# The next group's q1 turn in an attention loop: from a group's third step into its first

## The reference

```python
qkv = jnp.einsum('bsd,df->bsf', x, Wqkv) + bqkv
q, k, v = ...                       # 32, 8 and 8 heads of 8
k = jnp.repeat(k, N_REP, axis=2)    # N_REP = 4
v = jnp.repeat(v, N_REP, axis=2)
scores = jnp.einsum('bqhd,bkhd->bhqk', q, k) / np.sqrt(HEAD_DIM)
attn = jax.nn.softmax(scores, axis=-1)
out = jnp.einsum('bhqk,bkhd->bqhd', attn, v).reshape(bsz, seqlen, D_MODEL)
return jnp.einsum('bsd,de->bse', out, Wo) + bo
```

## Time and profile before

| | |
|---|---|
| median of 3 runs | 671.64 us (670.51 to 672.01) |
| profiled execution | 669.68 us |
| its span | 667.8 us, mean granted TensorE clock 0.986 of 2.4 GHz |
| attention loop of layer 1 | about 362 to 563 us in the span |
| TensorE busy (matmul) | 617.4 us, 92% of the span |
| VectorE busy | 404.4 us, 61% |
| ScalarE busy | 325.1 us, 49% |
| 256 maxima (L1744) | 681 ns each |
| 256 exponentials (L1505) | 598 ns each |

### The profile page before, as it was taken

The page is one execution under the profiler, slowest core; times in us unless marked ns, Lnnn a source line. Parts: engine busy times, 40 slices in busy tenths (PEclk is TensorE's granted clock), DMA queues, the critical chain, the costliest instruction groups (busy, mean ns, idle before and its releaser), DMA issues.

```text
span 667.8 us, 11795 instructions
## 1 busy us (share of the span) xinstructions
PE 617.4 (92%) x4298; PEld 408.0 (61%) x4298; DVE 404.4 (61%) x929; ACT 325.1 (49%) x645; POOL 213.2 (32%) x312
## 2 busy tenths in 40 slices
PE   3999999999999988799978999999999999989990
PEld 2887887887888785366665544444444445546660
DVE  4526705632760587533366999989998954743336
ACT  4523423433332224133215589898988875523322
POOL 5870561282073154513333031201010100331331
PEclk9999999999999999899989999999999999999996
DMA  6000200300199992222379994000000000031213
GB/s 220 33 1 33 96 1 20 107 1 1 38 283 299 78 314 77 78 58 81 105 237 346 303 180 3 1 1 2 2 1 2 1 2 1 9 104 55 81 56 126
DMA packets 69000, 57.40 MB, mean 86 GB/s; under 512 B 21520, under 2 KB 64400, under 8 KB 68944
## 3 DMA queue, kind: packets, MB, share of 16 engines
q1 hardware_dynamic: 66736, 50.60, 31.2%
q0 software_dynamic: 2208, 6.05, 2.5%
HBM read 30.78 MB, written 25.85 MB: 85 GB/s over the span
## 4 chain that ended last, share of the span: by engine, by line
PE 73%; DVE 16%; DMA 3%; ACT 3%; issue 2%; POOL 1%; SPq 1%; ACTq 0%; POOLq 0%; DVEq 0%
PE psum L303 9%; PE psum L305 8%; PE psum L304 8%; PE psum L1289 8%; PE psum L1634 8%; DVE mx L1744 7%; PE psum L1606 5%; PE psum L1318 5%; PE psum L1594 5%; PE psum L1619 3%; PE psum L1213 2%; DVE stat L666 2%; PE psum L1564 2%; PE psum L1282 2%; PE psum L1199 1%
## 5 line engine op out<-in xcount | busy, mean ns | idle before, releaser
L1744 DVE TENSOR_REDUCE mx<-psum 128x1 f32<-128x512 f32 x256 | 157.6, 681 | 17.6 <-PE psum L1606 17.5
L1505 ACT ACTIVATE pr<-psum 128x512 f32<-128x512 f32 x256 | 138.0, 598 | 27.9 <-PE psum L1619 26.1
L1634 PE MATMUL psum<-pr,vals 128*32 128x256 f32 x1024 | 77.6, 389 | 0.0
L1619 PE MATMUL psum<-qT,kT 32*128 32x512 f32 x256 | 76.6, 494 | 0.7 <-ACT pr L1505 0.7
L1606 PE MATMUL psum<-kT,qT 32*128 32x512 f32 x256 | 67.7, 488 | 1.7 <-ACT qT L1472 0.7
L1289 PE MATMUL psum<-w_gu,xgT 128*128 x120 | 56.4, 592 | 0.0
L624 POOL DMA_INDIRECT routed_y<-yr,xg x30 | 28.7, 958 | 86.1 <-DVE yr L876 85.5
L1606 PEld LDWEIGHTS psum<-kT,qT 32*128 32x128 f32 x256 | 26.3, 181 | 43.9 <-issue 21.4
L1546 POOL CAST mp<-mx 128x16 bf16<-128x16 f32 x16 | 3.1, 196 | 150.5 <-DVE mx L1744 150.5
L867 DVE SCALAR_TENSOR_TENSOR h<-psum,xg,sg 128x256 f32<-128x256 f32 x30 | 14.5, 484 | 49.8 <-ACT sg L1046 49.8
L1046 ACT ACTIVATE sg<-psum,xg 128x256 f32<-128x256 f32 x30 | 14.2, 474 | 60.4 <-PE psum L1289 60.4
(11 more groups left out here) (214 smaller groups left out, 1406.6 us busy)
## 6 DMA issues: line engine op xcount, KB each, us to landing
sorted_x<-zeros SPq DMA_DIRECT2D x2, 9088.0 KB, 39.2
w_gu<-in_L_ffn_gate_w SPq DMA_DIRECT2D x16, 256.0 KB, 6.2
w_gu<-in_L_ffn_up_w SPq DMA_DIRECT2D x16, 256.0 KB, 6.3
w_d<-in_L_ffn_down_w SPq DMA_DIRECT2D x16, 256.0 KB, 6.6
xg<-sorted_x SPq DMA_DIRECT2D x30, 129.0 KB, 2.2
wk_f<-in_L_attn_Wk SPq DMA_DIRECT2D x4, 512.0 KB, 5.2
wq_f<-in_L_attn_Wq SPq DMA_DIRECT2D x4, 512.0 KB, 6.0
wv_f<-in_L_attn_Wv SPq DMA_DIRECT2D x4, 512.0 KB, 3.7
```

Of the source, the lines that this page charges most:

```text
L1505: nc.scalar.activation(pr[d % 3][:, j], s2_bank(d, j), ACT.Exp, scale=SCALE).then_inc(exp_ready, 1)
L1619: mm(s2_bank(d, j), kT[n // GH][rows, kc * P:(kc + 1) * P], qT2[n % 2][rows, :], start=True, stop=True).then_inc(s2_made, 1)
L1634: last = mm(ps[AV_BANK][j * VW:(j + 1) * VW, cols], vals[:, n // NKV * TB + kc, n % NKV // GH * GH + j, :], pr[d % 3][:, j, cols], start=( ...
L1744: v.tensor_reduce(mx[n % 2][:, t, j:j + 1], s1_bank(c, j), AX.X, ALU.max, negate=True).then_inc(max_read, 1)
```

## The change

`turns_at` gave `q1` of the next group in a step 2, by itself. It now gives it in a step 0, ahead of the `o` turn. `q2` (step 1), `k` (step 3) and `o` (step 0) stay. For the first groups this means that `q1` of group 1 goes from step 2 to step 0, that of group 2 from step 6 to step 4, and so on to group 15, from step 58 to step 56. TensorE's and ScalarE's order and the ring `FOR_ACT` follow; VectorE's, GpSimd's and SyncE's orders are the same. The number of instructions is the same.

```diff
@@ -1369,14 +1369,14 @@
         def turns_at(c):
 
             if c % TB == 0:
-                what = ("o", (c - 12) // TB)
+                what = [("q1", c // TB + 1), ("o", (c - 12) // TB)]
             elif c % TB == 1:
-                what = ("q2", (c - 5) // TB)
-            elif c % TB == 2:
-                what = ("q1", c // TB + 1)
+                what = [("q2", (c - 5) // TB)]
+            elif c % TB == 3:
+                what = [("k", (c + 5) // 16 if (c + 5) % 16 == 0 else NG)]
             else:
-                what = ("k", (c + 5) // 16 if (c + 5) % 16 == 0 else NG)
-            return [what] if 0 <= what[1] < (NKT if what[0] == "k" else NG) else []
+                what = []
+            return [x_ for x_ in what if 0 <= x_[1] < (NKT if x_[0] == "k" else NG)]
```

## The result

The changed kernel takes 667.52 us (median of 20 runs) against 672.15 for the kernel before in the same comparison: ratio 0.9927, 95% interval 0.9908 to 0.9947, so 3.6 to 6.2 us less. The forecast was 667.8 us, 3.8 less than the 671.64 that it started from. That 667.8 and 667.52 lie so close is in part luck: 671.64 was the median of 3 runs, and the median of 20 is 0.5 higher. The profiled execution took 665.95 us, with a span of 664.2 against 667.8.

A forecast was written before the change was run, and what follows sets the result against it. Bound by the order of waits among three nearly full engines, step 2 paced by TensorE, step 0 by VectorE. 10 x 0.40 + 2 x 0.24 - 0.7 = 3.8 us off 671.64 gives 667.8 us, range 665.4 to 670.4.

The forecast's parts named there:

- Step 2 without the turn: Attention loop, step 2: with the q1 turn gone, VectorE's third maximum starts 0.42 us earlier and its wait disappears.
- TensorE until step 0: Steps 2 and 3: from step 2's start, step 0 begins 4.62 us later, step 3's last exponential ends 5.03 later.
- Step 0 with the turn: Step 0: TensorE's and VectorE's chains arrive together at the o turn, gaining 0.40 us a period, new period 10.90.
- no cover on ScalarE: Rival: ScalarE's exponentials don't move ahead, so step 0's o turn comes 0.13 us later; 673.9 us, chance 0.08.
- The wait moves: Rival: VectorE gains 0.42 us in step 2 but starves as long in step 0; some 672 us, chance 0.08.
- Its second form: Rival: VectorE held 0.68 us for each maximum, 16 filling 10.9 us, so no order could gain; chance 0.02.
- The groups with keys: Steps 27 and 43: the key turn in step 3 adds 0.59 us, period 11.49 against 11.73, gaining 0.24 each.
- The start: First groups of the loop: turns coming earlier cost 0.7 us together, bounds 0 and 1.2.
- Its part at step 8: Step 8's turn delays the weighing some 0.5 us, 0.2 is regained in step 10; 0.3 remains after step 12's turn.
- The part for steps 0 and 4: Turns ahead of the second pairs in steps 0 and 4: half a turn, 0.3 to 0.4 us, passes through.
- The sum: Whole loop: ten ordinary periods, two with keys and the start give 3.8 us less, 667.8 us.

## Why the prediction was right, step by step

- *Step 2 without the turn* (0.42, a wait less, a run of 14): as forecast; the last group of the kernel before was a true picture of it.
- *TensorE until step 0* (4.62 to the first pair, 5.03 to the last exponential's end): 461.05 - 456.44 = 4.61 and 5.03.
- *Step 0 with the turn* (0.40 a period, 10.90): 10.90. That two chains meet there is shown from both sides: 0.09 more on ScalarE costs 0.08, and taking the turn away gives 0.03, VectorE's limit. This also settles the rival *no cover on ScalarE*: its exponentials did move ahead with TensorE. Moved to where there was no such cover (behind the second pair, step 3), the same turn lost 0.2 to 0.3 of the 0.40 a period.
- *The wait moves*: not so in step 0, but in the run with the turn in step 3. Its second form, a VectorE held for each maximum's duration, is refuted by 14 maxima in 8.47 us: (8.47 - 0.68) / 13 = 0.60. The section "The DRAIN you can't avoid" of the Trainium skill's page "VectorE: DVE Perf Modes", by its sentence that the next operation doesn't start until the pipe is empty, would have said 0, if the recorded 0.68 is the time until then. The same section goes on "A next op that is not held starts earlier", which the prediction left out; the trace agrees with that, 0.60 from start to start beside 0.68.
- *The groups with keys* (11.49): 11.45 in the first; 11.74 in the second. Here the forecast held for the dependencies and missed 0.28 that isn't in them.
- *The start* (0.7): the term that was mis-sized, 0.34. Its part at step 8 was right: that weighing comes 0.53 later from step 3's projection on (0.49 by step 8's turn and 0.04 by step 4's, from the run with the early turns back: 14.69, 14.65 and 14.16), 0.32 comes back in the next period (11.75 before, 397.63 - 386.20 = 11.43 now), 0.2 remains where I had 0.3. The part for steps 0 and 4, 0.3 to 0.4, was 0.13 + 0.04; the 0.13 is 371.51 - 362.43 = 9.08 from the first scores to step 3's projection, 371.14 - 362.19 = 8.95 before. The step that failed reads "the idle of 0.28 in step 2 behind it says that half a turn passes through". It does get as far as step 2's first pair, which starts 5.59 behind the first scores and not 5.15 (368.02 - 362.43, 367.34 - 362.19). But the step leaves out that step 2 loses its own turn. Before, first the turn on TensorE and then what VectorE does behind it:

```profile
368.32 0.60 PE L1594 MATMUL psum<-ident,qs 128*128 128x128 f32 x4
```

```profile
369.38 3.68 DVE L1744 TENSOR_REDUCE mx<-psum 128x1 f32<-128x512 f32 x6 [0.21 <-PE psum L1606]
```

and VectorE in the changed kernel, from step 2's first maximum on:

```profile
368.55 4.88 DVE L1744 TENSOR_REDUCE mx<-psum 128x1 f32<-128x512 f32 x8 [0.40 <-PE psum L1606]
```

TensorE's second pair of step 2 is then as early as before (369.08 - 362.43 = 6.65, 368.85 - 362.19 = 6.66), and VectorE, 0.44 late at the first maximum, gets 0.30 back: its third maximum comes two steps of 0.60, 1.20, behind the first and not 369.38 - 367.88 = 1.50. 0.14 of the 0.44 passes through.
- *The sum*: ten periods of 0.40, 0.28 and -0.01 with keys, -0.34 at the start are 3.9. That this is so near to 3.8 is luck in part: the start cost 0.36 less than I had put it at, and the second group with keys gained 0.25 less, and the two all but cancel. From the first maximum (362.73 before, 362.96 after) to step 60's o turn (532.43 and 528.70), the two traces differ by 3.96. The spans differ by 3.6, since in the profile after, the loop begins 0.24 later (first scores at 362.43 and 362.19), ahead of anything that the change touches, and 0.1 went behind the loop. The medians' 4.6 is above what these two traces show, but the interval (3.6 to 6.2) takes both in.

What stays open: why an exponential at certain places in the queue starts 0.28 late, and why two adjacent turns take 0.16 less than two apart. Both are measured and neither is explained.

## What to carry to other kernels

When three engines are all near full, look for the step in which each waits for another, and move work that nobody is waiting for from a step paced by its engine to a step in which that engine waits; here the gain (0.40) was about what VectorE had lost behind the work in its old step (0.42), not the work's cost (0.59), and the wait in the new step decided how much of it was kept. The exact place inside the step matters almost as much as the step: behind the second pair instead of ahead of it, 0.23 of the 0.40 were gone, and in step 3 0.27. A group of the old trace that happens to lack the moved work, here the last one, is the best forecast of the rest.

## What was not expected of the hardware

Two turns in a row, eight 128x128 float32 transposes, took 1.02 us on TensorE up to the next scores, where two turns with other matmuls between took 0.59 each. A 128x1 copy on ScalarE lasted 0.21 us and moved what followed by 0.09. One exponential in the changed kernel started 0.28 us late for its place in ScalarE's queue alone: one instruction more ahead of it, and the delay was gone; 14 more, and another exponential had it. Moving the q2 turn behind its pair removed a 0.30 us wait of VectorE in step 1 and made the loop 0.37 a period slower: 0.24 of it because the move parted two pairs of matmuls that had run side by side, and VectorE waited longer elsewhere.
